# The experts of a mixture-of-experts kernel: rows prepared two experts ahead, the down product from three products of rounded parts, results copied by ScalarE into four buffers

## The reference, cut to what matters

```python
x = x + _L0_xattn_ref(_layernorm(x), ctx_2048, ...)
x = x + _L0_attn_ref(_layernorm(x), ...)
x = x + _L0_ffn_ref(_layernorm(x), gate_w, w_gate, w_up, w_down)

# _L0_ffn_ref: 64 experts, top 8 of each token, hidden 256, inner width 96
P = N * TOP_K
C = CAP_FACTOR * P // E                       # 512 rows per expert
scores, idx = jax.lax.top_k(softmax(x @ gate_w.T), TOP_K)
xbuf = zeros((E, C, D)).at[e_sorted, pos].set(x[tok_sorted], mode='drop')
g = einsum('ecd,efd->ecf', xbuf, w_gate)
u = einsum('ecd,efd->ecf', xbuf, w_up)
y = einsum('ecf,edf->ecd', silu(g) * u, w_down)
out = zeros((N, D)).at[tok_sorted].add(y[e_sorted, safe_pos] * (s_sorted * valid)[:, None])
```

## Time and profile before

| what | us |
|---|---|
| median of 3 runs (2297.53 to 2301.21) | 2300.67 |
| span of the profiled execution | 2296.0 |
| first `sg` of the expert loop to the last | 1871.2 to 2221.3 |
| first scatter (L1335) to the last | 1883.1 to 2237.4 |
| combine phase, after the barrier | from 2242.9 to the end |

### The profile page before, as it was taken

One profiled execution on the slowest core, in us unless ns is written; L12 is line 12 of the kernel. 1 busy time (PEld: TensorE's weight loads), 2 busy tenths in 40 slices (PEclk: granted clock), 3 DMA queues, 4 the chain that ended last, 5 costly groups with the idle time before them and its releaser, 6 DMA issues. The chain is left out here.

```text
span 2296.0 us, 56054 instructions
## 1 busy us (share of the span) xinstructions
PE 2102.5 (92%) x21448; PEld 1456.2 (63%) x21448; DVE 1751.3 (76%) x3728; ACT 1441.0 (63%) x3012; POOL 684.0 (30%) x646
## 2 busy tenths in 40 slices
PE   7999999999999999999999999999997149999975
PEld 5666666666666666666666666666664037777754
DVE  5557887979797978888888888797978736656646
ACT  2667676768676767676777767676867124444433
POOL 1002040404131322213130404040403427767770
PEclk9999999999999999999999999999999569999998
DMA  7586672323132313232323323232310136676648
GB/s 226 192 288 210 235 250 75 114 82 89 72 89 72 93 70 91 77 83 79 100 88 82 97 64 105 55 105 68 107 47 25 56 119 212 199 229 209 201 138 331
DMA packets 132711, 294.16 MB, mean 128 GB/s; under 512 B 21899, under 2 KB 89143, under 8 KB 126304
## 3 DMA queue, kind: packets, MB, share of 16 engines
q1 hardware_dynamic: 114016, 255.89, 35.7%
q0 software_dynamic: 18432, 34.69, 4.3%
HBM read 165.40 MB, written 108.27 MB: 119 GB/s over the span
## 5 line engine op out<-in xcount | busy, mean ns | idle before, releaser
L801 ACT ACTIVATE sb_probs<-S,sb_negmax 128x1604 f32<-128x1604 f32 x256 | 409.2, 1598 | 278.5 <-DVE sb_negmax L979 277.0
L793 ACT ACTIVATE sb_probsT<-W 128x384 f32<-128x384 f32 (+1 forms) x1024 | 473.6, 513 | 68.2 <-PE W L639 65.3
L639 PE MATMUL W<-sb_ident,sb_probs 128*128 128x128 f32 (+1 forms) x3328 | 478.3, 280 | 15.7 <-DVE sb_o_tok L992 8.0
L979 DVE TENSOR_REDUCE sb_negmax<-S 128x1 f32<-128x1604 f32 x256 | 466.2, 1821 | 2.9 <-PE S L629 1.2
L639 PEld LDWEIGHTS W<-sb_ident,sb_probs 128*128 128x128 f32 (+1 forms) x3328 | 363.5, 139 | 133.9 <-issue 64.7
L612 PE MATMUL W<-sb_wkv_in,sb_ctx 128*128 128x256 f32 (+1 forms) x1664 | 410.7, 389 | 14.2 <-ACT sb_probsT L793 6.6
L602 PE MATMUL W<-sb_ctx,sb_wkv_in 128*32 128x401 f32 x4096 | 399.3, 504 | 4.4 <-DVE sb_V L973 2.9
L612 PEld LDWEIGHTS W<-sb_wkv_in,sb_ctx 128*128 128x128 f32 (+1 forms) x1664 | 293.3, 187 | 79.1 <-ACT sb_probsT L793 25.7
L1335 POOL DMA_INDIRECT y_scratch<-sb_ys,sb_places x256 | 264.4, 1033 | 112.1 <-issue 109.0
L963 DVE SCALAR_TENSOR_TENSOR sb_K_lo<-W,sb_pair_cols,sb_K_hi 128x401 fp32r<-128x401 f32 x256 | 162.2, 633 | 175.5 <-ACT sb_K_hi L785 175.2
L785 ACT ACTIVATE sb_K_hi<-W,sb_pair_cols 128x401 fp32r<-128x401 f32 x256 | 153.2, 598 | 181.5 <-PE W L602 181.4
(11 more groups left out here) (188 smaller groups left out, 2921.0 us busy)
## 6 DMA issues: line engine op xcount, KB each, us to landing
sb_ctx<-ctxT SPq DMA_DIRECT2D x32, 1604.0 KB, 7.7
xe_scratch<-sb_none SPq DMA_DIRECT2D x32, 1088.0 KB, 12.7
sb_xg<-xe_scratch SPq DMA_DIRECT2D x64, 544.0 KB
sb_BC<-bc_scratch SPq DMA_DIRECT2D x32, 1024.0 KB, 5.9
sb_Q_hi<-sb_q_hi SPq DMA_DIRECT2D x128, 128.0 KB, 4.5
sb_Q_lo<-sb_q_lo SPq DMA_DIRECT2D x128, 128.0 KB, 5.4
y_scratch<-sb_none SPq DMA_DIRECT2D x16, 1024.0 KB, 12.0
sb_rows<-y_scratch SPq DMA_DIRECT2D x16, 1024.0 KB, 8.1
```

The lines of the kernel that those rows point to most:

```text
L639: ins = pe.transpose(W[0:keys_in(t), at * P:(at + 1) * P], probs[n % 2][:, t * P:t * P + keys_in(t)], ident[:])
L793: act.activation(probsT[k][n % (k + 1)][:, 0:wide], ring[bank_of("T", G, k)][:, 0:wide], ACT.Copy)\
L801: act.activation(probs[n % 2][:].rearrange("p (c k) -> p c k", c=QUADS), scores_of, ACT.Exp, bias=negmax[:, slot:slot + 1], accum_out=den[ ...
L979: dve.tensor_reduce(negmax[:, slot:slot + 1], scores_of, AX.XY, ALU.max, negate=True).then_inc(max_done, 1)
```

## The change

Four things change, all in `expert_phase`.

1. Rows are turned and parted two experts ahead (`AHEAD = 2`): the loop body e does `gate_up(e)`, `turn(e+2)`, `down(e-1)` on PE and `split(e+2)` on ACT and DVE. Two experts are prepared before the loop. SP's loads follow: rows and weights of e+2 are issued in body e.
2. The down product is made as gate and up are: ACT rounds `wd` and `hid` (`wd_hi`, `hid_hi`), DVE subtracts (`wd_lo`, `hid_lo`), and PE forms 12 matmuls of rounded parts in place of 4 in float32. On ACT `split_down(e)` stands between silu and `split(e+2)`; on DVE between `split(e+2)` and `find_places(e+2)`. `hid` keeps one buffer, its parts have two.
3. ACT alone copies the whole result `Y` (now one tensor) to `ys`; DVE's copy goes. POOL waits for one semaphore (`y_up`) in place of two.
4. `ys` has four buffers and `places` eight: the copy of expert e waits for the rows of expert e-4.

```diff
+        AHEAD = 2
+        DEEP = 4
+        PLACES = 2 * DEEP
...
-        hid = [sb(f"hid{n}", [FF, CAP]) for n in range(2)]
-        ys = [sb(f"ys{n}", [P, CT, D]) for n in range(2)]
+        hid = sb("hid", [FF, CAP])
+        hid_hi, hid_lo = ([sb(f"hid_{m}{n}", [FF, CAP], F32R) for n in range(2)] for m in ("hi", "lo"))
+        wd_hi, wd_lo = ([sb(f"wd_{m}{n}", [FF, D], F32R) for n in range(2)] for m in ("hi", "lo"))
+        ys = [sb(f"ys{n}", [P, CT, D]) for n in range(DEEP)]
...
-        Y = [ctx.enter_context(nc.psum_tensor(f"Y{k}", [P, 2, D], F32)) for k in range(2)]
+        Y = ctx.enter_context(nc.psum_tensor("Y", [P, CT, D], F32))
...
         @block.sync
+            def load_d(e):
+
+                after(sp, down_lo_up, e - 1)
+                sp.dma_start(wd[e % 2][:], io["wdT"][e:e + 1].rearrange("o f d -> (o f) d")).then_inc(wd_in[e % 2], 16)
+
+            for e in range(AHEAD):
+                load_x(e)
+                load_gu(e)
+            for e in range(E):
+                if e + AHEAD < E:
+                    load_x(e + AHEAD)
+                    load_gu(e + AHEAD)
                 if e == X3_AT:
...
-                after(sp, y_done, e - 1)
-                sp.dma_start(wd[n][:], io["wdT"][bass.ds(e, 1)].rearrange("o f d -> (o f) d")).then_inc(wd_in[n], 16)
+                load_d(e)
...
         @block.gpsimd
                 pool.wait_ge(places_up, e + 1)
-                for m in range(2):
-                    pool.wait_ge(y_up[m], e + 1)
+                pool.wait_ge(y_up, e + 1)
...
         @block.tensor
-            def down(e, n):
-                pe.wait_ge(hid_up, e + 1)
-                pe.wait_ge(wd_in[n], in_count(e, n))
-                for m in range(2):
-                    after(pe, y_up[m], e)
-                for c in range(CT):
-                    ins = pe.matmul(Y[c // 2][:, c % 2, :], hid[n][:, c * P:(c + 1) * P], wd[n][:], start=True, stop=True)
+            def down(e):
+                pe.wait_ge(down_lo_up, e + 1)
+                after(pe, y_up, e)
+                products = ((hid_hi, wd_hi), (hid_lo, wd_hi), (hid_hi, wd_lo))
+                for c in range(CT):
+                    for p, (h, w) in enumerate(products):
+                        ins = pe.matmul(Y[:, c, :], h[e % 2][:, c * P:(c + 1) * P], w[e % 2][:],
+                                        start=(p == 0), stop=(p == len(products) - 1))
                 ins.then_inc(y_done, 1)
...
+            for e in range(AHEAD):
+                turn(e)
+            for e in range(E):
+                gate_up(e)
+                if e + AHEAD < E:
+                    turn(e + AHEAD)
+                if e > 0:
+                    down(e - 1)
+            down(E - 1)
...
         @block.scalar
+            def split_down(e):
+                act.wait_ge(wd_in[e % 2], in_count(e))
+                after(act, y_done, e - 1)
+                act.activation(wd_hi[e % 2][:], wd[e % 2][:], ACT.Copy).then_inc(wd_hi_up, 1)
+                act.wait_ge(hid_up, e + 1)
+                act.activation(hid_hi[e % 2][:], hid[:], ACT.Copy).then_inc(hid_hi_up, 1)
+
+            def out(e):
                 act.wait_ge(y_done, e + 1)
-                if not early(e):
-                    act.wait_ge(y_out[n], (e - n) * 8 * CT)
-                act.activation(ys[n][:, 0:2, :], Y[0][:], ACT.Copy).then_inc(y_up[0], 1)
+                after(act, y_out[e % DEEP], rows_out(e))
+                act.activation(ys[e % DEEP][:], Y[:], ACT.Copy).then_inc(y_up, 1)
...
                 act.activation(sg[:], G[0:FF, :], ACT.Silu).then_inc(sg_up, 1)
+                split_down(e)
+                if e + AHEAD < E:
+                    split(e + AHEAD)
+                if e > 0:
+                    out(e - 1)
...
         @block.vector
+            def split_down(e):
+                dve.wait_ge(wd_hi_up, e + 1)
+                dve.tensor_tensor(wd_lo[e % 2][:], wd[e % 2][:], wd_hi[e % 2][:].bitcast(F32), ALU.subtract)
+                dve.wait_ge(hid_hi_up, e + 1)
+                dve.tensor_tensor(hid_lo[e % 2][:], hid[:], hid_hi[e % 2][:].bitcast(F32), ALU.subtract).then_inc(down_lo_up, 1)
...
-                dve.tensor_copy(ys[n][:, 2:4, :], Y[1][:]).then_inc(y_up[1], 1)
...
                 dve.wait_ge(gu_done, e + 1)
                 dve.wait_ge(sg_up, e + 1)
-                after(dve, y_done, e - 1)
-                dve.tensor_tensor(hid[n][:], U[0:FF, :], sg[:], ALU.mult).then_inc(hid_up, 1)
+                after(dve, down_lo_up, e)
+                dve.tensor_tensor(hid[:], U[0:FF, :], sg[:], ALU.mult).then_inc(hid_up, 1)
+                if e + AHEAD < E:
+                    split(e + AHEAD)
+                split_down(e)
+                if e + AHEAD < E:
+                    find_places(e + AHEAD)
```

More of the change, by code:

```diff
@@ L1240, in expert_phase @@
         place = sb("place", [P, CT])
-        places = [sb(f"places{n}", [P, CT], U32) for n in range(4)]
+        places = [sb(f"places{n}", [P, CT], U32) for n in range(PLACES)]
         wgu = [sb(f"wgu{n}", [P, DT, 2 * FF]) for n in range(2)]
@@ L1267, in expert_phase @@
         hid_up = sem("hid_up")
+        hid_hi_up = sem("hid_hi_up")
+        wd_hi_up = sem("wd_hi_up")
+        down_lo_up = sem("down_lo_up")
         y_done = sem("y_done")
-        y_up = [sem("y_up_act"), sem("y_up_dve")]
-        y_out = [sem(f"y_out{n}") for n in range(2)]
+        y_up = sem("y_up")
+        y_out = [sem(f"y_out{n}") for n in range(DEEP)]
         match_up = sem("match_up")
@@ L1274, in expert_phase, with in_count @@
         block = ctx.enter_context(nc.Block())
[L1276 to L1292, removed]
+        def in_count(e):
+            return 16 * (e // 2 + 1)
@@ L1381, in body @@
-            def body(e, n):
-                gate_up(e, n)
-                if not last(e):
-                    turn(e + 1, 1 - n)
-                if not first(e):
-                    down(e - 1, 1 - n)
-            over_experts(pe, body)
-            down(E - 1, (E - 1) % 2)
+            for e in range(AHEAD):
+                turn(e)
+            for e in range(E):
+                gate_up(e)
[3 more added lines that the diff above has]
+                    down(e - 1)
@@ L1391, in _, with split @@
+            down(E - 1)
         @block.scalar
         def _(act):
-            def split(e, n):
-                act.wait_ge(wgu_in[n], in_count(e, n))
+            def split(e):
+                act.wait_ge(wgu_in[e % 2], in_count(e))
                 after(act, gu_done, e - 1)
-                act.activation(w_hi[n][:], wgu[n][:], ACT.Copy).then_inc(w_hi_up, 1)
+                act.activation(w_hi[e % 2][:], wgu[e % 2][:], ACT.Copy).then_inc(w_hi_up, 1)
                 for k in range(DT):
@@ L1400, in split @@
                     act.wait_ge(xt_done, DT * e + k + 1)
-                    act.activation(x_hi[n][:, k, :], XT[k][:], ACT.Copy).then_inc(x_hi_up, 1)
-            def out(e, n):
-                act.wait_ge(y_done, e + 1)
-                if not early(e):
-                    act.wait_ge(y_out[n], (e - n) * 8 * CT)
-                act.activation(ys[n][:, 0:2, :], Y[0][:], ACT.Copy).then_inc(y_up[0], 1)
-            def body(e, n):
+                    act.activation(x_hi[e % 2][:, k, :], XT[k][:], ACT.Copy).then_inc(x_hi_up, 1)
@@ L1410, in body @@
+            for e in range(AHEAD):
+                split(e)
+            for e in range(E):
                 act.wait_ge(g_done, e + 1)
@@ L1439, in find_places @@
                 dve.tensor_reduce(place[:], match[:], AX.X, ALU.add).then_inc(place_sum, 1)
[L1440 to L1441 removed]
+                if e >= PLACES:
+                    dve.wait_ge(y_out[e % DEEP], rows_out(e - DEEP))
                 dve.wait_ge(place_sum, e + 1)
[L1443 to L1451 removed]
+                dve.tensor_scalar(places[e % PLACES][:], place[:], float(NO_PLACE), None, ALU.add).then_inc(places_up, 1)
+            for e in range(AHEAD):
+                split(e)
+                find_places(e)
+            for e in range(E):
                 dve.wait_ge(gu_done, e + 1)
                 dve.wait_ge(sg_up, e + 1)
[L1455 to L1466 removed]
+                after(dve, down_lo_up, e)
[5 more added lines that the diff above has]
+                    find_places(e + AHEAD)
 def combine_phase(nc, io, dram, out):
```

75 lines of the change are left out of this document (22 added, 53 removed).

## The result

The changed kernel takes 2284.07 us (median of 5 runs, 2281.97 to 2285.17) against 2299.89 of the kernel before in the same session: a ratio of 0.9926, 95% interval 0.9914 to 0.9937. It is faster by 0.74%, about 16 us, where 11 us more were predicted. Its profiled execution took 2283.78, with a span of 2282.0.

The account below looks back on a forecast made before the run. PE's 5.48 us step bounds the kernel before, with POOL falling behind; afterwards POOL's 5.11 plus 0.54 of holds makes 5.65. 60 x 0.17 = +10.2 gives 2306 profiled, 4.7 below the median of runs: 2311, range 2290 to 2335.

Parts of the forecast that it names:

- PE: PE's step per expert: 12 down products at 0.12 us, 1.44 together, bring it from 5.48 to 5.14 (5.01 to 6.34).
- ACT's copy: ACT's copy of the whole result, 1024 columns, costs about 1.02 us, beside PE.
- start: Start of the loop: turn(1) costs about 2 us, the second gate_up regains it; taken at 0, plus or minus 2.
- DVE: DVE's loop per expert: hid, the wait for ACT and the queued operations sum to 5.15 us, a little less with overlaps.
- the rival of whole scatters: Rival: a scatter holds DVE for its whole 0.97, 1.1 us per expert; DVE's loop 6.25, time 2347; chance 0.03.
- the hold of 0.54 added to 5.11: POOL's scatters: holds by w_lo (0.23) and wd_lo with hid_lo (0.31) lengthen its free step of 5.11 to 5.65 us.
- 8 places per 5.11 us: POOL's four scatters have two places each where DVE can hold them, one per 0.64 us.
- a random phase: DVE operations meet the scatters' places by chance: 0.54/0.64 for w_lo, which then holds 0.27 us on average.
- PE decides after all: Rival: holds nearly vanish, step is PE's 5.14 or DVE's 5.15, 20 us less, 2281; needs holds under 0.04; chance 0.07.
- SP: Loads issued about a step earlier, past nothing new and hidden by the step of 5 us: costed at nothing.
- Four buffers: Result buffers let POOL fall two experts further behind before ACT must wait; they do not shorten a scatter.
- the second place: A scatter can be held at its start and again some 0.7 us in; w_lo inside one lengthened it to 1.18.

Follow-up runs that it names:

- two_products_scatter3: Changed kernel without the third down product (hid_hi x wd_lo) and without each expert's fourth scatter: 2278.18 us, ratio 0.9909.
- w_hi_first: x3_last with ACT rounding the gate and up weights before waiting for hid, and DVE's w_lo and down parts moved ahead of its x parts: 2279.99 us.
- hid128: Changed kernel with hid, hid_hi and hid_lo on 128 partitions instead of 96: 2285.61 us, ratio 0.9931.
- scatter5: Changed kernel with a fifth scatter per expert, group 0's rows again into a second DRAM tensor: 2363.56 us, ratio 1.0261.
- hidlo_twice: Changed kernel with DVE's subtraction hid_lo made twice, first into a spare tile: 2318.30 us, ratio 1.0082.
- x3_last: Changed kernel with the 2 MB load issued behind the last expert's loads instead of in the middle of the loop: 2274.60 us, ratio 0.988.
- f32_down: Changed kernel with the float32 down product back, without the parts of hid and wd on ACT and DVE: 2291.79 us, ratio 0.997.
- before_four_buffers: Kernel before with only the change's four result buffers and eight lists of places: 2299.88 us, ratio 0.9987.
- two_buffers: Changed kernel with two result buffers and four lists of places instead of four and eight: 2311.66 us, ratio 1.0051.

## Why the prediction was wrong

**PE: right.** 12 products at 0.12, a step of 5.08 for 5.14. **ACT's copy** at 1.02 and the **start** at 0 were right too; the first scatter is 0.4 later.

**DVE: right in size, not taken seriously.** "5.15, a little less as starts overlap" became 5.065 of its own and 5.125 with the 0.065 by which a scatter lengthens `wd_lo`. The prediction gave the waits on DVE no term of their own, only the rival of whole scatters with 1.1 per expert. Relieved of that scatter, the step falls to 5.06 (two_products_scatter3); with DVE's chain made shorter, to PE's 5.09 (w_hi_first).

**POOL, the step that failed: the hold of 0.54 added to 5.11.** Two things were wrong in it.

First, its size. "8 places per 5.11 us" counted two places per scatter, the second from `w_lo` inside a scatter. In the changed kernel and its variants, but for the two scatters of hid128, there is only the one at the start. With that rule an operation of length L holds a scatter that starts while it runs, and for less than its length: of scatters that come every 1.277 at random, about (L - 0.15)^2 / 2 / 1.277 per operation (0.15: the operation must have started some 0.03 before the scatter, and its end must come more than 0.97 - 0.85 = 0.12 after that start). By this estimate it is 0.07 + 0.03 + 0.11 = 0.20 for `w_lo`, `wd_lo`, `hid_lo`. Where POOL set the pace, 0.14 (w_hi_first) and 0.25 (the profiled execution of scatter5; less in the other) were measured.

Second, and this turned the sign: a random phase was assumed where POOL would set the pace, but POOL's free step (5.11) lies just below DVE's with its wait (5.125). An engine with the shorter loop catches up until something stops it, and here the stop is the hold itself. In most steps of the changed kernel a scatter starts as `w_lo` is about to end (1942.26 against 1942.40, 0.98 long), and of the other starts only that at 1943.55 is covered, 0.02 behind the start of `wd_lo` and so too early to be held [timeline above]. This phase also makes the wait that keeps DVE above POOL: the scatter behind a held one starts 0.85 + 0.30 = 1.15 after the end of `w_lo`, `wd_lo` 1.13 after it, so the two start together and `wd_lo` is lengthened. By their own loops alone (5.065 and 5.11) POOL would be the slower one, and holds would be added as the prediction has it, though smaller ones. That the two keep to this phase is what the rows show; why they come into it was not tested. The hold settles at the slack: 0.37 in the second half of the kernel before, 0.015 in the changed kernel, 0.62 in hidlo_twice. In the first and the last it adds nothing; in the changed kernel the step is 0.015 over POOL's free one. The prediction had this very sentence for the kernel before ("falls back until the hold makes its step equal to that of PE") and did not ask it of the kernel after. The rival "PE decides after all", at 0.07, came nearest: the holds under 0.04 that it demanded are what is seen, only it is DVE with its wait, not PE, that has the longest loop.

The margin is thin: with a step 0.015 above POOL's 5.11 the holds all but vanish (x3_last, 2274.6), with one 0.02 below it they cost 0.14 per expert (w_hi_first, 2280.0), by one profile of each.

By the Trainium skill, page "SBUF — State Buffer", section "SBUF: two separate sides", whichever starts first of a GpSimd operation and a DVE operation with two SBUF inputs keeps the shared ports for its whole instruction and the other fully blocks. For DVE first, by 0.04 or more, the runs agree: a scatter ends 0.85 after the operation does. For a scatter first they do not: `wd_lo`, started with one, lasts 0.065 longer and is not kept out for 0.97, and `hid_lo` 0.38 into it takes its usual 0.68.

**SP: costed at nothing, cost 5.9.** The prediction named what hides the moved loads, but not what stands behind the 2 MB load in SP's order: the down weights of the same expert, which `split_down` now wants right behind silu and not a body later. At that load 10.3 us of steps are lost instead of 4.4; f32_down, where the down weights are again wanted a body later, loses 4.9 there. x3_last takes all of it away (9.5 us by the medians).

**Four buffers: half right.** They shorten no scatter (before_four_buffers), but the change could not do without the eight lists (two_buffers, 27.6 us).

Open is the second place: in the kernel before, `w_lo` begun 0.38 into a scatter lengthens it to 1.18; in no variant of the changed kernel does it, not even in w_hi_first, where `w_lo` follows `hid` as closely. There `w_lo` takes 0.56, before it takes 0.54; what the difference is was not found. The place is not a fixed point inside the scatter: in the kernel before and in before_four_buffers, 83 of the 85 scatters that start under `hid` end 0.80 after the start of the `w_lo` behind it (if that is later than their 0.97), and none of the 51 such scatters of f32_down and w_hi_first is lengthened. The two long scatters of hid128, also behind two operations in a row, may be the same thing; it was not followed further.

## What to carry to other kernels

When two engines hold each other up at a shared resource, do not add holds at random phase to the slower loop. Write down each engine's loop twice, by itself and with what the other costs it. Where one loop is clearly shorter, its engine slides until the hold eats its slack and no more (hidlo_twice, the second half of the kernel before); where the held engine is the slowest, holds cost time (w_hi_first, scatter5); where the loops differ by less than the waits, as here, the phase in which they settle decides, and only a run tells. So a tuning that makes the other engines faster than the held one can lose, as w_hi_first did by its profile. And when a consumer of a load is moved earlier, look at what is queued ahead of that load on its issuing engine, and at every list that must live longer, not only at the buffers of the data.

## What the hardware showed unexpectedly

- In the changed kernel and its variants a scatter of 128 rows has one point at which a DVE operation with two SBUF inputs holds it: at its start. If the operation has then run for 0.04 or more, the scatter ends 0.85 after it; an operation that starts with the scatter or after it does not lengthen it. Two scatters of hid128 and the kernel before go against this.
- The other way round a scatter costs DVE little: `wd_lo` takes 0.477 instead of 0.41 where it starts with one, 0.065 per expert of four scatters.
- One more wait in the program ahead of `places` made DVE's step 0.1 longer, from the list on at which it begins.
- Behind 2 MB issued as one load, ACT waited 10.3 us for the next 96 KB load on SP; at the end of the loop the same load cost nothing that the step or the end of the scatters shows.
